# Macaron layer on one core: half-batches instead of batches, quads of heads, fp32 value product in column strips

## Chip, cores, metric

One core of a Trainium2 chip runs the whole program. The metric is device time in microseconds (us), the median of the runs shown.

## What is computed

The input is x with 4 batches of 1024 tokens and 128 features, all in fp32. Three layers follow each other, each on the normalised x:

```python
x = x + 0.5 * ffn(layernorm(x), router_w, router_b, expert_weights)   # first layer, "f = 0"
x = x + attn(layernorm(x), wq, wk_down, wv_down, wk_up, wv_up, wo)    # attention
x = x + 0.5 * ffn(layernorm(x), ...)                                  # last layer, "f = 1"

# ffn: softmax over 8 experts, the best 2, weights normalised; all 8 products x @ E[e] and a gated sum
# attn: 8 query heads of 128, 2 key heads; keys and values are x @ down (32 wide) @ up (32 x 128);
#       causal softmax(q k / sqrt(128)) v, then y @ wo
```

## The kernel before, in words

Keys and values are 32 wide ahead of their up projection, so the kernel folds the up projections into wq and wo. A score then has a contraction of 32, and precision comes from splitting each fp32 factor in a high part (float32r) and a low one: q_stack holds hi, lo, hi of a query head on 96 partitions, k_stack holds hi, hi, lo of a key head. Partitions 96 and 97 of q_stack hold the row maximum (high and low part), those of k_stack hold -1, so that the score matmul subtracts the maximum.

The work of a batch in attention is 96 score blocks: 8 heads, and in each head 12 blocks of 128 keys by up to 512 queries (BLOCKS; 512, 384, 256 or 128 columns, mean 384). For a block there are these steps:

- `maximum` (L1142, and a mask matmul L1145 on the diagonal) makes scores in the other orientation (128 queries by up to 512 keys) in one of 3 banks; the VectorE reduction L935 takes the row maximum into m_part.
- When a head has its 12 maxima, L928 merges them, TensorE transposes them (L1196), ScalarE copies twice (L586), GpSimd takes the low part (L556), and two DMAs put the row into q_stack (L465).
- `scores` (L1157, mask L1160) in one of 2 banks, then ScalarE's exponential L682 into prob (9 buffers of 128 x 512 fp32).
- The low half of prob: prob_lo = prob - upper bf16 half, by GpSimd (L562, three quarters of the blocks) or VectorE (L951).
- `values` (L1180 and L1181): for each 128 queries of the block one matmul with the bf16 upper half of prob as stationary operand and one with the fp16 low half, 97 moving columns each (three bf16 parts of the 32 value columns, and a column of ones that gives the denominator). 36 pieces of 128 queries in a head, so 72 of these matmuls a head and 576 a batch. They accumulate in bank OB; after the last block of 512 queries VectorE makes the reciprocal (L920), the sum of the three parts (L921) and the product (L943, y_lat).

After a batch, `join` transposes y_lat (L1266), ScalarE copies it (yT), and L1277 multiplies with wo; VectorE adds x1_kept (L1009).

The order of the work is written out by hand. Every engine runs the same list of slots, one slot for each of the 96 score blocks (`timeline`, L220 and following), with the offsets of all other steps given in slots: maxima run 20 slots ahead (MAX_LEAD), the row of a head 6 ahead, values 5 to 7 behind. `front(k + 1)` puts the first layer and the projections of the next batch in the slots of batch k, `join` and `back(k - 1)` the output projection and the last layer of the batch before. Batches 1 and 2 are a hardware loop (Fori), batches 0 and 3 are written out; before the first slot comes the whole front of batch 0, and after the last the whole join and back of batch 3.

The first and last layer (ffn) work on tiles of 128 tokens, 8 a batch: statistics (L770, L781), the power and shift by GpSimd (L524, L526), ScalarE's normalisation (L622), transposes (L1079), high and low part, router matmuls (L1101, L1102, 16 and 8 columns), 26 small VectorE instructions for the gates (L820, one set a batch), then two jobs a tile with three float32r matmuls of 512 columns each (L1084 to L1086). ScalarE scales four experts (L661), VectorE adds four (L878), GpSimd joins the sums (L538, L541, L543). The two banks FB serve all of it.

SyncE issues the DMAs that build q_stack and k_stack (L443, L455): 3 a query head and 3 a key head, 30 a batch.

In `prepare_rest` (L1052) stands the only place where matmuls write strips of 32 partitions side by side:

```python
for h in range(NH):
    g, r = divmod(h, NR)
    last = mm(bank[4][r * DL:(r + 1) * DL, g * D:(g + 1) * D], upT[:, DL:2 * DL], wo_sb[:, h, :],
              start=True, stop=True)
```

Of the kernel before, what the change touches and what calls it, by code (L numbers as in the profile page):

```python
# [5 lines left out]
F32 = mybir.dt.float32  # L21
F32R = mybir.dt.float32r
BF16 = mybir.dt.bfloat16
FP16 = mybir.dt.float16
# [5 lines left out]
P = 128  # L30
NT = T // P
CH = 512
NC = T // CH
TC = CH // P
NE = 8
NH, NKV, DL = 8, 2, 32
NR = NH // NKV
NU = NH * NC
# [7 lines left out]
VCOLS = 3 * DL + 1  # L46


BLOCKS = [(c, j) for c in range(NC) for j in range(TC * (c + 1))]

MBLOCKS = [(i, k) for i in range(NT) for k in range(i // TC + 1)]
NBL = len(BLOCKS)
NS = NH * NBL
GS = NS // NKV

MAX_LEAD = 20
ROW_LEAD = 6
PV_LAG = 5
PV_HOLD = 2
NORM_LAG = PV_LAG + 1  # L60
NP = 9

# [4 lines left out]

CUT = 4
JOIN = 7
JOIN_OUT = 11
OUT_STEP = 1
KEEP = 11
STACK_1 = 5
STACK_EVERY = 2
VALUES_1 = 10

BN = [8, 0, 42]  # L80
STATS = [10, 55, 45]
POWER = [12, 55, 47]
XN = [13, 59, 49]
XT = [16, 62, 52]
XHI = [17, 63, 52]
XLO = [17, 64, 53]
XT_STEP = 2

LOGITS = [21, 57]
LOGITS_STEP = [0, 0]  # L90
ROUTE = [22, 59]
ROUTE_SLOTS = [3, 10]
GATE_EXP = [24, 58]
Y = [26, 74]
PACE = [3, 3]
PICK_ACT = 1
PICK_DVE = 1
SPREAD = 0
FINISH = 2
TILE_STATS = 4  # L100

LOAD = 4
PROJ = 68
QUERIES = 69
VALUES = 74
STACK_0 = QUERIES + 3
VALUES_STEP = 0
VALUES_0 = VALUES + 2

HALF = NE // 2  # L110
STAT_SLOTS = 2
# [3 lines left out]
JOBS = 2 * NT  # L115
# [3 lines left out]
def last_block(u):  # L119

    h, c = divmod(u, NC)
    return h * NBL + (TC - 1 if c == 0 else NBL - 1)


UNIT_ENDS = {last_block(u): u for u in range(NU)}


def offset(s):

    c, j = BLOCKS[s % NBL]  # L130
    return max(0, j - TC * c) * P


def diagonal(s):

    c, j = BLOCKS[s % NBL]
    return j >= TC * c


def on_pool(s):  # L140

    return s % NBL not in (0, 3, 6)


def splits(s, pool):

    return sum(on_pool(i) == pool for i in range(s + 1))


def values_slot(s):  # L150

    n = BLOCKS[s % NBL][1]
    return s + max(0, PV_HOLD - n) + PV_LAG


def job_slot(f, j):

    return Y[f] + j // 2 * PACE[f] + j % 2 * (PACE[f] // 2)


def job_at(f, s):

    return next((j for j in range(JOBS) if job_slot(f, j) == s), None)

ENTRIES = []
for _m in range(NS):
    if _m % NBL == MAX_LEAD - NBL - ROW_LEAD:  # L170
        ENTRIES.append(("row", _m // NBL - 1))
    ENTRIES.append(("block", _m))
ENTRY = {e: n for n, e in enumerate(ENTRIES)}


def maxima_bank(entry):

    return MX + ENTRY[entry] % NMX


def entry_before(entry):

    n = ENTRY[entry]
    for back_by in range(1, len(ENTRIES)):
        other = ENTRIES[(n - back_by) % len(ENTRIES)]
        if maxima_bank(other) == maxima_bank(entry):
            return other, back_by > n


def at(k, s):  # L190

    return k + s // NS if s // NS else k, s % NS


def real(b):

    return not isinstance(b, int) or 0 <= b < NB


def is_first(b):  # L200

    return isinstance(b, int) and b == 0


def job_banks(b, f):

    alone = isinstance(b, int) and b == (NB - 1 if f else 0)
    return [FB, FB + 1, MX, MX + 1] if alone else [FB, FB + 1]


def job_bank(b, f, j):
    banks = job_banks(b, f)
    return banks[j % len(banks)]


def need(engine, semaphore, value):

    if not isinstance(value, int) or value > 0:
        engine.wait_ge(semaphore, value)


def timeline(engine, slot, front, join, back):

    for s in range(CUT, CUT + NS):
        front(0, s)

    def run(k, lo, hi):
        for s in range(lo, hi):
            slot(k, s)
            if s >= CUT:  # L230
                if real(k - 1):
                    join(k - 1, s)
                if real(k + 1):
                    front(k + 1, s)
                if real(k - 1):
                    back(k - 1, s)

    run(0, -MAX_LEAD, CUT + NS)
    with engine.Fori(1, NB - 1) as k:
        run(k, CUT, CUT + NS)  # L240
    run(NB - 1, CUT, CUT + NS)
    for s in range(CUT, CUT + NS):
        slot(NB, s)
        join(NB - 1, s)
        back(NB - 1, s)


def macaron(nc, x, wq, wk_down, wv_down, wk_up, wv_up, wo, router_w, router_b, experts, out):
    ctx = ExitStack()
    with ctx:  # L250
# [11 lines left out]

# [3 lines left out]
        mask_kq = sb("mask_kq", [P, P], BF16)  # L266
        rank = sb("rank", [P, NE])
        half_power = sb("half_power", [P, NT])

        wk_up_sb = sb("wk_up_sb", [DL, D])  # L270
        wv_up_sb = sb("wv_up_sb", [DL, D])
        down_sb = sb("down_sb", [P, 2 * NKV * DL])
        rw_sb = sb("rw_sb", [NE, D])
        rb_sb = sb("rb_sb", [P, NE])
        we_sb = sb("we_sb", [P, NE * D])
# [9 lines left out]
        wo_lat = sb("wo_lat", [P, NKV, D])  # L285

        x0 = sb("x0", [P, NT, D])
        x1 = sb("x1", [P, NT, D])
        x1_kept = sb("x1_kept", [P, NT, D])
        x2 = sb("x2", [P, NT, D])  # L290
        x3 = sb("x3", [P, NT, D])
# [109 lines left out]
        def per_expert(ap):  # L401

            return ap.unsqueeze(2).to_broadcast([P, NT, NE])
# [907 lines left out]
```

## Time and profile before

| | us |
|---|---|
| median of 3 runs | 710.64 |
| lowest and highest | 705.13 and 713.25 |
| span of the profiled execution, which is its own time too | 705.1 |
| TensorE / VectorE / GpSimd / ScalarE busy in it | 584.4 / 527.5 / 390.9 / 332.5 |
| mean granted TensorE clock | 0.872 |

The span runs from the first to the last instruction. A TensorE matmul's busy time holds its way through the array too, so the distance between the starts of two matmuls that follow each other says more than a duration. The lines of the page are those of kernel.py.

### The profile page before, as it was taken

The numbers are of one execution on the slowest core, as the hardware profiler recorded it, in microseconds if no ns is written. First come the engines' busy times: TensorE is split into PE (matmuls) and PEld (weight loads), VectorE is DVE, ScalarE is ACT, GpSimd is POOL, SyncE is SP. The second block draws the span as 40 slices with busy tenths as digits, with TensorE's granted clock in tenths as the row PEclk, the third lists the DMA queues.
The fourth block names the chain that finished last, engine by engine and source line by source line (L and its number), as shares of the span: only waits on it lengthen the run. The fifth ranks groups of instructions, "written<-read, shape, count | busy, mean of one in ns | idle before, by whom it ended". The sixth has DMA issues, their size and how long they took to land.

```text
span 705.1 us, 14707 instructions
## 1 busy us (share of the span) xinstructions
PE 584.4 (83%) x4627; PEld 443.5 (63%) x4627; DVE 527.5 (75%) x1454; ACT 332.5 (47%) x885; POOL 390.9 (55%) x549
## 2 busy tenths in 40 slices
PE   3847988989978989888898989888899888898475
PEld 3624666766757856666677756666677667675353
DVE  3553789996788899986796899895787897865243
ACT  4344154655534546553464555554364455355133
POOL 2160164986446549652685559652676575469206
PEclk9986589997989999878898999878699998799857
DMA  4002350000313300004106100003105100000000
GB/s 125 1 1 63 75 148 1 2 2 1 91 24 81 96 2 2 1 2 91 24 3 153 55 1 2 1 2 91 24 3 121 53 2 2 2 2 0 31 0 30
DMA packets 18525, 24.93 MB, mean 35 GB/s; under 512 B 3144, under 2 KB 13968, under 8 KB 18448
## 3 DMA queue, kind: packets, MB, share of 16 engines
q1 hardware_dynamic: 15328, 22.40, 12.9%
q10 hardware_dynamic: 3120, 1.57, 0.8%
q8 instruction: 40, 0.66, 0.4%
q14 instruction: 37, 0.30, 0.1%
HBM read 3.78 MB, written 2.10 MB: 8 GB/s over the span
## 4 chain that ended last, share of the span: by engine, by line
POOL 30%; issue 22%; PE 21%; DVE 19%; ACT 5%; DMA 1%; POOLq 1%; SPq 1%; ACTq 0%; DVEq 0%
POOL prob_lo L562 15%; DVE m_part L935 5%; POOL pair_sum L538 5%; POOL pair_sum L541 4%; PE bank L1142 4%; PE bank L1157 3%; PE bank L1180 3%; PE bank L1181 2%; POOL x L543 2%; POOL rstd L524 2%; DVE prob_lo L951 2%; ACT xn L622 2%; DVE y_lat L943 2%; DVE dve_sum L878 1%; PE bank L1084 1%
## 5 line engine op out<-in xcount | busy, mean ns | idle before, releaser
L562 POOL TENSOR_TENSOR prob_lo<-prob 128x512 f16<-128x512 f32 (+3 forms) x288 | 237.1, 840 | 178.1 <-ACT prob L682 177.5
L682 ACT ACTIVATE prob<-bank 128x512 f32<-128x512 f32 (+3 forms) x384 | 182.8, 487 | 212.0 <-PE bank L1160 191.9
L935 DVE TENSOR_REDUCE m_part<-bank 128x1 f32<-128x512 f32 (+3 forms) x384 | 207.7, 548 | 81.8 <-PE bank L1142 48.2
L1142 PE MATMUL bank<-k_stack,q_stack 96*128 96x512 f32 (+3 forms) x384 | 168.5, 446 | 13.5 <-DVE m_part L935 12.1
L1157 PE MATMUL bank<-q_stack,k_stack 98*128 98x512 f32 (+3 forms) x384 | 166.9, 436 | 8.3 <-ACT prob L682 5.0
L1180 PE MATMUL bank<-v_parts,prob 128*128 128x97 bf16 x1152 | 151.2, 225 | 14.3 <-DVE y_lat L943 13.2
L1181 PE MATMUL bank<-v_parts,prob_lo 128*128 128x97 bf16 x1152 | 149.8, 223 | 0.0
L1180 PEld LDWEIGHTS bank<-v_parts,prob 128*128 128x128 bf16 x1152 | 116.0, 108 | 34.0 <-issue 12.2
L1181 PEld LDWEIGHTS bank<-v_parts,prob_lo 128*128 128x128 f16 x1152 | 117.1, 108 | 0.0
L1142 PEld LDWEIGHTS bank<-k_stack,q_stack 96*128 96x128 f32 x384 | 86.3, 225 | 23.6 <-DVE m_part L935 20.4
L1157 PEld LDWEIGHTS bank<-q_stack,k_stack 98*128 98x128 f32 x384 | 81.5, 212 | 17.5 <-ACT prob L682 6.8
L661 ACT ACTIVATE scaled<-bank,gate 128x128 f32<-128x128 f32 x256 | 72.1, 367 | 28.6 <-POOL x L543 16.5
L1084 PE MATMUL bank<-we_hi,xT_hi 128*128 128x512 f32 x128 | 65.2, 509 | 16.3 <-DVE dve_sum L878 7.7
L538 POOL TENSOR_TENSOR pair_sum<-dve_sum,scaled 128x256 f32<-128x256 f32 x64 | 47.5, 742 | 53.8 <-DVE dve_sum L878 53.8
L951 DVE TENSOR_TENSOR prob_lo<-prob 128x512 f16<-128x512 f32 (+1 forms) x96 | 66.1, 688 | 5.9 <-ACT prob L682 5.8
L1145 PE MATMUL bank<-mask_qk,ident_b 128*128 128x128 bf16 x256 | 64.2, 251 | 0.0
L1160 PE MATMUL bank<-mask_kq,ident_b 128*128 128x128 bf16 x256 | 62.6, 245 | 0.0
L1085 PE MATMUL bank<-we_lo,xT_hi 128*128 128x512 f32 x128 | 54.3, 424 | 0.0
L1086 PE MATMUL bank<-we_hi,xT_lo 128*128 128x512 f32 x128 | 53.9, 421 | 0.0
L622 ACT ACTIVATE xn<-x,shift,rstd 128x128 f32<-128x128 f32 x96 | 40.9, 484 | 25.1 <-POOL shift L526 25.1
L1145 PEld LDWEIGHTS bank<-mask_qk,ident_b 128*128 128x128 bf16 x256 | 27.3, 107 | 35.7 <-issue 26.4
L1160 PEld LDWEIGHTS bank<-mask_kq,ident_b 128*128 128x128 bf16 x256 | 26.6, 104 | 33.9 <-issue 23.4
(132 smaller groups left out, 847.7 us busy)
## 6 DMA issues: line engine op xcount, KB each, us to landing
q_stack<-q_hi SPq DMA_DIRECT2D x64, 128.0 KB, 2.4
q_stack<-q_lo SPq DMA_DIRECT2D x32, 128.0 KB, 2.4
k_stack<-k_hi SPq DMA_DIRECT2D x16, 128.0 KB, 2.5
x_kept<-x SPq DMA_DIRECT2D x4, 512.0 KB, 3.3
out_x<-x SPq DMA_DIRECT2D x4, 512.0 KB, 3.9
x<-in_L_attn_x ACTq DMA_DIRECT2D x3, 512.0 KB, 4.0
k_stack<-k_lo SPq DMA_DIRECT2D x8, 128.0 KB, 2.4
x<-in_L_attn_x SPq DMA_DIRECT2D x1, 512.0 KB, 4.0
```

The source lines that it names most:

```text
L538: nc.gpsimd.tensor_tensor(pair, dve_sum[:, t % 2, 1:3], scaled[:, t % 2, 2:4], ALU.add)\
L562: nc.gpsimd.tensor_tensor(prob_lo[:, ls % NP, 0:w], prob[:, ls % NP, 0:w], upper_half(ls, w), ALU.subtract).then_inc(split_done[True], 1)
L682: nc.scalar.activation(prob[:, ls % NP, 0:w], bank[ST + ls % NST][:, 0:w], ACT.Exp, scale=SCALE).then_inc(p_ready, 1)
L935: V.reduce_max(m_part[:, h, kc, i:i + 1], bank[maxima_bank(("block", ls))][:, 0:w], AX.X)\
L951: V.tensor_tensor(prob_lo[:, ls % NP, 0:w], prob[:, ls % NP, 0:w], upper_half(ls, w), ALU.subtract).then_inc(split_done[False], 1)
L1084: mm(dst, lhs[0], rhs[0], start=True, stop=False)
L1142: last = mm(into[:, 0:w], q_stack[0:MROW, h, i * P:(i + 1) * P], k_stack[0:MROW, h // NR, kc * CH:kc * CH + w], start=True, stop=not diagonal)
L1145: last = mm(into[:, w - P:w], ident_b[:], mask_qk[:], start=False, stop=True)
L1157: last = mm(bank[ST + ls % NST][:, 0:CH - off], k_stack[:, h // NR, j * P:(j + 1) * P], q_stack[:, h, c * CH + off:(c + 1) * CH], start=Tr ...
L1160: last = mm(bank[ST + ls % NST][:, 0:P], ident_b[:], mask_kq[:], start=False, stop=True)
L1180: mm(acc, hi[:, n * P:(n + 1) * P], v, start=first and i == 0, stop=False, skip_group_check=True)
L1181: last = mm(acc, prob_lo[:, ls % NP, n * P:(n + 1) * P], v, start=False, stop=final and i == TC - 1, skip_group_check=True)
```

## The change

The hardware loop goes; all slots are written out, from -70 to 436, with score blocks in slots 0 to 383. The first and last layer and the projections work by half-batches (8 "chunks" n of 512 tokens), each with its own start slot. Attention works by quads, the four heads of one key head for one half of the queries: 4 quads a batch, with 4 or 8 key tiles each, and within a quad key tile by key tile, the four heads one after the other:

```diff
-BLOCKS = [(c, j) for c in range(NC) for j in range(TC * (c + 1))]
+QUADS = [(c, g) for c in range(NC) for g in range(NKV)]
+QTILES = [TC * (c + 1) for c, g in QUADS]
+NPG = 4
+PV_LAG = 3
+ACC_LAG = 2
+DIRECT = 2
...
+def front_start(n):
+    b, c = divmod(n, NC)
+    if b == 0:
+        return (-68, -54)[c]
+    return (b - 1) * NS + (-6, 40)[c]
+
+def back_start(n):
+    b, c = divmod(n, NC)
+    if b == NB - 1:
+        return b * NS + (46, 108)[c]
+    return b * NS + (64, NS + 18)[c]
+
+def join_slot(n):
+    b, c = divmod(n, NC)
+    return b * NS + (40, 104)[c]
```

Relative to its start a chunk has its statistics at +0, the router at +10, the jobs of its four tiles from +15 to +25, and in the front the key projection at +38, the queries at +39 and +40, the values at +41.

The product with the values (TensorE) takes the fp32 probabilities as moving operand and the fp32 values (32 columns) as stationary one; the four heads of a key tile write the four strips of 32 partitions of one bank. prob_lo, v_parts and their instructions are gone:

```diff
-                    mm(acc, hi[:, n * P:(n + 1) * P], v, start=first and i == 0, stop=False, skip_group_check=True)
-                    last = mm(acc, prob_lo[:, ls % NP, n * P:(n + 1) * P], v, start=False,
-                              stop=final and i == TC - 1, skip_group_check=True)
+            def weighted_values(b, q, j):
+                c, g = QUADS[q]
+                off = first_query(q, j)
+                if j == 0:
+                    need(pe, o_copied, b * NQ + q)
+                    pe.wait_ge(v_ready, b * NC + c + 1)
+                pe.wait_ge(p_ready, group_end(b, q, j) + 1)
+                for r in range(NR):
+                    last = mm(bank[OB][r * DL:(r + 1) * DL, off:CH], v_lat[:, b % 2, j, g, :],
+                              probabilities(b, q, j, r), start=j == 0, stop=j == QTILES[q] - 1)
+                last.then_inc(pv_done, 1)
```

The denominators: GpSimd adds the groups of probabilities (key tile 1 up to the third last) into that of key tile 0, two heads in an instruction; TensorE multiplies that sum and the last two groups with a block of ones, in the same four strips, in one of the three banks of the maxima; VectorE transposes 32 x 32 blocks, makes 16 reciprocals a partition and transposes back; ScalarE copies the values' bank, and GpSimd multiplies into yT. With this y_lat and its transposes are gone:

```diff
+            def add_group(b, q, j):
...
+                for half in range(2):
+                    heads = slice(2 * half, 2 * half + 2)
+                    pool.wait_ge(p_ready, group_end(b, q, j) - 1 + 2 * half)
+                    if j > 1:
+                        pool.wait_ge(sum_step, 2 * k - 1 + half)
+                    into = acc[:, (b * NQ + q) % 2, heads, off:CH]
+                    nc.gpsimd.tensor_tensor(into, into, prob[:, home, heads, 0:CH - off], ALU.add)\
+                        .then_inc(sum_step, 1)
...
+            def denominators(Q):
...
+                for j in [0] + list(range(nj - DIRECT, nj)):
+                    for r in range(NR):
+                        last = mm(into[r * DL:(r + 1) * DL, first_query(q, j):CH], ones[:], probabilities(b, q, j, r),
+                                  start=j == 0, stop=j == nj - 1)
...
+                if step == 0:
+                    dve.wait_ge(den_done, Q + 1)
+                    V.transpose(den_t[:], mx_bank(("den", Q))[:]).then_inc(den_step, 1)
```

The maxima of a quad (16 blocks, or 32) have one row step instead of one a head, with one ScalarE copy and the low part by VectorE; they run 38 slots ahead of the batch's first score for three quads, and the fourth quad's in slots 26 to 57. q_stack and k_stack are filled by half-batches, 60 DMAs a batch of half the size each.

## Rows read from the trace of the kernel before

In rows 1 and 10 a line is a stretch: start and end, length, then busy us (and instructions) of TensorE's matmuls, its weight loads, VectorE, ScalarE and GpSimd, then the granted TensorE clock (1 is 2.4 GHz, 0.5 is 1.2 GHz), the DMA share and GB/s. The edges in rows 1 are the starts of the first score matmul of a batch, but for 649 us, which is behind the last.

**Rows 1.** Stretches: prelude, batch 1, batch 3, tail.

```profile
0.00:81.80 81.80, 51.91 (x201) 35.90 (x201) 41.90 (x141) 26.95 (x71) 19.56 (x42) 0.83 0.20 52
...
234.60:392.00 157.40, 138.34 (x1149) 105.87 (x1149) 130.61 (x360) 80.96 (x220) 97.31 (x135) 0.89 0.15 37
...
550.00:649.00 99.00, 87.35 (x788) 66.46 (x788) 76.11 (x199) 49.05 (x129) 63.47 (x83) 0.88 0.03 8
649.00:705.10 56.10, 30.38 (x142) 22.93 (x140) 22.04 (x84) 16.95 (x51) 20.41 (x37) 0.76 0.06 19
```

**Rows 2.** Timeline of TensorE at 301 us: start, duration, line, tile.

```profile
301.63 0.48 PE L1142 MATMUL bank<-k_stack,q_stack 96*128 96x512 f32 x1
301.95 0.22 PE L1157 MATMUL bank<-q_stack,k_stack 98*128 98x128 f32 x1
302.01 0.23 PE L1160 MATMUL bank<-mask_kq,ident_b 128*128 128x128 bf16 x1
...
302.33 0.21 PE L1180 MATMUL bank<-v_parts,prob 128*128 128x97 bf16 x1
302.37 0.21 PE L1181 MATMUL bank<-v_parts,prob_lo 128*128 128x97 bf16 x1
```

**Rows 3.** The same view at 32 us (experts) and 659 us (output projection).

```profile
32.05 0.50 PE L1084 MATMUL bank<-we_hi,xT_hi 128*128 128x512 f32 x1
...
32.86 0.40 PE L1084 MATMUL bank<-we_hi,xT_hi 128*128 128x512 f32 x1
...
659.11 3.84 PE L1277 MATMUL bank<-wo_lat,yT 128*128 128x128 f32 x32 [0.71 <-ACT yT L586]
```

**Rows 4.** Timeline at 24 us: the 16 matmuls of prepare_rest in four strips.

```profile
23.87 0.35 PE L1102 MATMUL bank<-rw_parts,xT_lo 128*128 128x8 f32 x1
...
24.16 1.08 PE L1052 MATMUL bank<-x,upT 128*32 128x128 f32 x16
...
26.19 0.63 PE L1086 MATMUL bank<-we_hi,xT_lo 128*128 128x512 f32 x1
26.61 0.63 PE L1084 MATMUL bank<-we_hi,xT_hi 128*128 128x512 f32 x1
```

**Rows 5.** The same timeline, only those in flight from 24.16 to 24.20 us.

```profile
24.16 0.44 PE L1052 MATMUL bank<-x,upT 128*32 128x128 f32 x4
```

**Rows 6.** Timeline at 318 us: from 128 columns of the array to 64.

```profile
318.02 0.28 PE L1181 MATMUL bank<-v_parts,prob_lo 128*128 128x97 bf16 x1
318.08 0.67 PE L1084 MATMUL bank<-xT_hi,down_hi 128*64 128x512 f32 x1
```

**Rows 7.** Groups by shape on GpSimd and VectorE: count, busy us, mean ns, idle before.

```profile
L562 POOL TENSOR_TENSOR prob_lo<-prob 128x512 f16<-128x512 f32 x128 | 134.0, 1060 | 83.4 <-ACT prob L682 83.3
L562 POOL TENSOR_TENSOR prob_lo<-prob 128x128 f16<-128x128 f32 x32 | 12.8, 400 | 6.2 <-ACT prob L682 5.9
L921 DVE TENSOR_REDUCE o_sum<-bank 128x128 f32<-128x384 f32 x64 | 33.4, 522 | 0.0
L943 DVE TENSOR_TENSOR y_lat<-o_sum,rden 128x128 f32<-128x128 f32 x64 | 33.3, 520 | 1.5 <-PE bank L1266 1.3
```

**Rows 8.** The page's group of VectorE's share of prob_lo.

```profile
L951 DVE TENSOR_TENSOR prob_lo<-prob 128x512 f16<-128x512 f32 (+1 forms) x96 | 66.1, 688 | 5.9 <-ACT prob L682 5.8
```

**Rows 9.** Waits: total us, times, longest.

```profile
PEld bank L1142 <- DVE m_part L935: 20.4, 33, 3.7
PE bank L1180 <- DVE y_lat L943: 13.2, 14, 2.0
PEld bank L1180 <- POOL prob_lo L562: 11.9, 15, 2.1
```

**Rows 10.** Short stretches around the projections, columns as in rows 1.

```profile
324.00:331.00 7.00, 7.00 (x80) 5.74 (x78) 5.37 (x10) 3.21 (x7) 2.41 (x4) 1.00 0.51 116
...
334.60:341.00 6.40, 6.40 (x36) 4.56 (x34) 4.04 (x14) 4.18 (x14) 2.54 (x3) 0.81 0.06 12
```

**Rows 11.** Timeline of SyncE: the issue of one stack DMA.

```profile
327.95 0.59 SPq L443 DMA_DIRECT2D q_stack<-q_hi  x1
```

More of the change, by code:

```diff
@@ L34 @@
 TC = CH // P
+NN = NB * NC
 NE = 8
@@ L114 @@
 N_DMA = 16
-JOBS = 2 * NT
+JOBS = 2 * TC
 CONST_STEPS = 9
[L119 to L153, printed above, removed]
@@ L156, in job_slot @@
[L156 to L187, printed above, removed]
@@ L190, in at @@
[L190 to L213, printed above, removed]
+BN, STATS, POWER, XN, XT, XHI, XLO, LOGITS, ROUTE, GATE_EXP, Y = 0, 1, 3, 5, 7, 8, 9, 10, 11, 12, 15
@@ new lines, in start_of, with chunks_at, quad_of, score @@
+def start_of(f, n):
+    return back_start(n) if f else front_start(n)
+PHASES = sorted(((f, n) for f in range(2) for n in range(NN)), key=lambda p: start_of(*p))
+PHASE = {p: i for i, p in enumerate(PHASES)}
+def chunks_at(f, s, step):
+    return [n for n in range(NN) if start_of(f, n) + step == s]
+def quad_of(ls):
+    return max(q for q in range(NQ) if QSTART[q] <= ls)
+def score(n):
+    b, ls = divmod(n, NS)
+    q = quad_of(ls)
+    j, r = divmod(ls - QSTART[q], NR)
+    return b, q, j, r, max(0, j - TC * QUADS[q][0]) * P
@@ L216, in need @@
+MX_USE = {u: i for i, u in enumerate(MX_USES)}
+FB_USE = {u: i for i, u in enumerate(FB_USES)}
 def need(engine, semaphore, value):
-    if not isinstance(value, int) or value > 0:
+    if value > 0:
         engine.wait_ge(semaphore, value)
[L222 to L245, printed above, removed]
@@ L1012, in back @@
-            def back(b, s):
-                if s == BN[2]:
-                    dve.wait_ge(x2_ready, (b + 1) * NC)
-                norm_piece(b, 2, x2, s)
-                expert_piece(b, 1, s, x2, x3)
-            timeline(dve, slot, front, join, back)
+                        dve.wait_ge(dve_picked, tile * HALF + 1)
+                    V.scalar_tensor_tensor(out=sums[e % 3], in0=fb_bank(("y", f, n, 2 * t + 1))[:, e * D:(e + 1) * D],
+                                           scalar=gate[:, f, n % 2, t, HALF + e:HALF + e + 1], in1=addends[e],
+                                           op0=ALU.mult, op1=ALU.add).then_inc(dve_picked, 1)
@@ L1281, in back, with scores @@
-            def back(b, s):
-                norm_piece(b, 2, s)
-                for c in range(NC):
-                    if s == LOGITS[1] + c * LOGITS_STEP[1]:
-                        router(b, 1, 2, c)
-                if job_at(1, s) is not None:
-                    expert_products(b, 1, job_at(1, s))
-            timeline(pe, slot, front, join, back)
+            def scores(n):
+                b, q, j, r, off = score(n)
+                c, g = QUADS[q]
+                if j == 0 and r == 0:
+                    pe.wait_ge(m_row[q], (b + 1) * 2 * N_DMA)
+                need(pe, p_ready, n - NST + 1)
+                into = bank[ST + n % NST]
+                last = mm(into[:, 0:CH - off], k_stack[:, b % 2, g, j * P:(j + 1) * P],
+                          q_stack[:, c, g * NR + r, off:CH], start=True, stop=not on_diagonal(q, j))
+                if on_diagonal(q, j):
+                    last = mm(into[:, 0:P], ident_b[:], mask_kq[:], start=False, stop=True)
+                last.then_inc(st_done, 1)
```

1349 lines of the change are left out of this document (658 added, 691 removed).

## Prediction

> **What bounds the kernel now.** I read the stretches first, since one mean over the span mixes three regimes [rows 1]: 81.8 us until the first score, three batches of 152.8, 157.4 and 158.0 us (the starts are 81.8, 234.6, 392.0 and 550.0), a last one of 99.0 that has no front to carry, and 56.1 us of tail. In a middle batch TensorE's records cover 138 of 157 us, VectorE's 131, GpSimd's 97, ScalarE's 81. Then the timeline, since a matmul's record is longer than the time in which it blocks the next. At 2.4 GHz starts lie 0.32 us apart behind a score of 512 columns, 0.06 behind one of 128, and 0.04 for the 97 columns of a value matmul, though their records last 0.48, 0.22 and 0.21 [rows 2]. An expert job of three matmuls takes 0.81, a small fp32 matmul 3.84 / 32 = 0.12 [rows 3].
>
> A middle batch by these distances: 576 value matmuls x 0.043 = 24.8 us; 192 scores and maxima, by width 96 x 0.32, 64 x 0.22 (my interpolation for 384 and 256 columns) and 32 x 0.06 = 46.7; 128 masks x 0.045 = 5.8; 32 expert jobs x 0.81 = 25.9; twelve projections of 512 columns x 0.25 and about 128 small matmuls (router, value projection, both kinds of transposes, output) x 0.115 = 17.7. Sum 121 us at full clock. At a granted clock of 0.89 the 157.4 us hold 140 us of full-clock time. So TensorE works 121 of 140, stands 19, and the half clock costs another 17. TensorE bounds the middle; the ends are bound by latency (VectorE 42 and TensorE 52 busy of 81.8, 22 and 30 of 56.1).
>
> The waits that make up the 19 are in part removed by the change [rows 9]: the values wait 13.2 us for y_lat and 11.9 for prob_lo, the maxima 20.4 for VectorE's reductions. Low clock follows stretches of few columns: from 324 to 331 us, at clock 1, the value projection with its 64-column matmuls ends; from 334.6 on it is 0.81 [rows 10].
>
> **The change on TensorE.** It removes 24.8 us of values and 16 transposes of y_lat x 0.115 = 1.8. It adds 96 value matmuls of fp32, in 24 groups of four strips. Do strips run side by side? In prepare_rest four are in flight together, 0.44 us for all four [rows 5], and 16 take 1.08 [rows 4]: (1.08 - 0.44) / 3 = 0.213 us for each round of four. The three-pass neighbours show the low clock there, 0.42 us for 512 columns (26.19 to 26.61) [rows 4], so 128 columns are 0.107 and a round is two cycles a column. A source matmul is two instructions (8 in the source, 16 in the row), so a group of four heads costs four cycles a column: 0.85 us for 512 columns at 2.4 GHz. Columns a batch: quads of 4 key tiles 512 + 384 + 256 + 128 = 1280, of 8 tiles 2048 + 1280 = 3328, together twice each 9216, x 4 / 2.4 = 15.4 us. Denominators: 512 + 256 + 128 = 896 columns a quad, 4 quads, 6.0 us. Bound from the other side: strips in series, four times both.
>
> Entering strips: L1102 starts at 23.87, the strips at 24.16 [rows 4], 0.29 where 0.21 is its own distance at that clock; from full width to 64 columns 318.02 to 318.08 is 0.06 [rows 6], less than the 0.08 of its columns. I take 0.15 us for each of 28 groups (24 and 4), in and out together, 4.2 us; bounds 0 and 0.4 (a record's length beyond its columns, 0.21 - 0.04, twice [rows 2]), so 0 to 11. New load: 121 - 24.8 - 1.8 + 15.4 + 6.0 + 4.2 = 120 us. The value product is no cheaper for the array; the gain must come from waits, clock and ends.
>
> The Trainium skill, TensorEngine Tiling (Array Packing), Key Properties, says that changing the tiling mode drains TensorE. The trace shows 0.08 us and nothing for two such changes [rows 4, 6], so I keep the sum; what the rule would do here at the upper bound's price is rival D.
>
> **The other engines, a middle batch.** VectorE: less 66.1 / 4 = 16.5 for prob_lo [rows 8], 33.4 / 4 + 33.3 / 4 = 16.7 for o_sum and y_lat [rows 7], about 10 for reciprocals, v_parts and m_fin (estimate from their counts, 8 to 64 short ones); plus two transposes of 512 columns a quad at 0.7 (as prob_lo's mean of 0.69 [rows 8]; bounds 0.52, as o_sum, and twice 0.7), 6 us, and the doubled count of small gate and statistic instructions, 73 x 0.2 = 15. 131 - 43 + 22 = 110. GpSimd: an add of two heads has 1024 or 768 elements; 1060 ns for 512 and 400 for 128 give 1.72 ns an element [rows 7], so 1.94 and 1.5 us (bounds: twice 1.06 and twice that again, if fp32 output or VectorE's port slows it). A batch has 16 long and 8 short ones, 43 us. Removed are 72 splits of 384 columns in the mean, 0.40 + 256 x 0.00172 = 0.84 each, 60 us, and eight low parts of a row at about 0.5. With normalise (four of 512 elements, 4.2) and more power steps (3, estimate) it ends near 97 - 64 + 50 = 83. ScalarE keeps its exponentials, near 80. None of the three passes TensorE. SyncE goes from 30 to 60 stack DMAs a batch at 0.59 [rows 11], 36 us of issue, beside everything. Behind a chunk's 30 DMAs (18 us, some 13 slots) waits the row of the next quad; rows are asked for 5 to 21 slots ahead of their scores, so I count 0, and 5 us a batch if the queue is late.
>
> Added waits: values wait for a whole group of exponentials, 3 slots behind the last, behind them on TensorE the next scores; 3 slots are 4 us against 0.6 for an exponential, hidden. The exponential of a group waits for GpSimd's add of the group 4 back, 12 slots later. Where tiles finish (three GpSimd instructions of 256, 128 and 128 elements, by the same line 0.6 + 0.4 + 0.4 = 1.4 us every 3 slots) and 8-tile quads are summed (3.9 every 4 slots), GpSimd needs 5.8 us in 4 slots of 1.5, about all of them, but only for 12 slots at a time, and the four buffers hold that.
>
> **The period.** Full-clock idle 19: less (13.2 + 11.9) / 4 = 6.3 for the removed waits, less half of 20.4 / 4 as VectorE falls from 0.83 of the period to 0.76, plus 2 for the denominators' and quads' hand-overs: 12. Router and value projection come in halves, with scores between, so stretches of few columns are shorter; I put the clock at 0.91 (bounds 0.75 and 0.97). (120 + 12) / 0.91 = 145 us against 152.8 to 158.0.
>
> **The ends.** Prelude: routing and experts of chunk 1 stand ahead of chunk 0's projections in the order, and the first quad needs 18 DMAs (11 us) and 16 maxima where a head needed 6 and 12. Half the first layer saved, about as much put back: 78 (bounds 70 to 88) for 81.8. Last batch: less than 99.0, since more maxima lie ahead, though chunk 6's last layer is now in it: 96. Tail: 56.1 falls to four tiles: statistics, eight transposes less, four experts less (about 2 us a tile, estimate from two jobs of 0.81 [rows 3] and their hand-over) but the whole gate chain; 39 (34 to 46).
>
> Sum 78 + 3 x 145 + 96 + 39 = 648 for the profiled execution. It has 705.1 where the median is 710.64, 5.5 more; forecast 654.
>
> **Rivals.**
> A, the forecast, 0.43: 625 to 682.
> B, 0.20: the waits only change their names and the clock stays; (120 + 19) / 0.89 = 156 a batch, 78 + 468 + 100 + 39 = 685, 690 with the offset. For it: PE's expert banks and the order of the slots stay, and VectorE stays at 0.7 to 0.8.
> C, 0.13: 6 idle at 0.97 is 130; 78 + 390 + 86 + 38 = 592, 597. For it: no wait in the middle is needed by the loads; against: 0.89 in every batch.
> D, 0.08: each change of width drains the array, at the 0.17 us that a record runs beyond its columns [rows 2]: 11 us with the rounding up a batch in place of 4.2: (127 + 14) / 0.91 = 155; 692 at the end.
> E, slower, 0.12: TensorE falls to the low clock while it runs strips and small groups between short waits. At 0.75 a batch takes (120 + 12) / 0.75 = 176: 78 + 528 + 116 + 40 = 762, 767. It turns the sign from a mean clock of about 0.82 down, where 132 / 0.82 = 161 eats what the ends give. For it: the clock drops behind few-column stretches [rows 10]; against: rounds of strips move as many columns a cycle as full-width ones.
> F, slower, 0.04: the strips run in series because 512 columns of fp32 from four buffers differ from 128 of one; 64 us more a batch, over 900. Against: rows 5.
>
> **Chances.** Faster by over 1%: A, C, nearly all of B and D, 0.79; within 1% 0.06 (the upper edge of B and D; about what a measurement can tell); slower 0.15. Range 594 to 718: below lies 0.05 of C, above E and F. A's own is 625 to 682.
>
> **What would show it.** In the profile after: value groups 0.85 us apart for 512 columns at clock 1, eight instructions each (else F); no gap over 0.15 at their edges (else D); mean clock in the middle 0.9 (else E); GpSimd's 1024-element add near 1.94 us; VectorE 110 a batch; batch starts 145 apart; first score at 78, 39 from last score to end. If periods of 156 appear with the loads as worked out, the idle term was wrong.

## The result and the profile after

The changed kernel takes 798.68 us (median of 4, 792.26 to 802.26) where the kernel before, run beside it, takes 707.88 (median of 4, 699.29 to 713.25): a ratio of 1.130, 95% interval 1.124 to 1.136. The forecast was 654 with a range up to 718. The sign was wrong and the range did not hold the time. All times below leave out the executions of a second, slower state (a lower granted clock and a longer time, whatever the kernel), so that den_pe stands at 746.4 us and tiny_rows at 708.0 where the expectations name the medians of all their executions, 752.95 and 708.87.

The stretches of the profiled execution of the changed kernel (span 800.4 us), cut at the first score of each batch and at the last score; columns as in [rows 1]:

```profile
0.00:100.00 100.00, 54.19 (x216) 37.82 (x216) 50.03 (x189) 28.36 (x74) 22.29 (x47) 0.78 0.26 67
100.20:266.80 166.60, 138.24 (x779) 82.45 (x779) 122.43 (x317) 72.84 (x186) 80.73 (x72) 0.84 0.10 23
266.80:454.60 187.80, 156.43 (x840) 95.03 (x839) 130.18 (x362) 79.97 (x211) 89.84 (x89) 0.78 0.11 28
454.60:637.50 182.90, 155.36 (x841) 94.69 (x840) 125.16 (x351) 79.97 (x210) 85.69 (x85) 0.78 0.11 26
637.50:753.00 115.50, 102.03 (x642) 57.80 (x641) 67.52 (x185) 59.54 (x146) 68.84 (x58) 0.88 0.06 15
753.00:800.00 47.00, 20.56 (x90) 13.22 (x86) 14.05 (x58) 7.96 (x24) 15.60 (x19) 0.68 0.02 6
```

For a comparison the kernel before has to be divided in the same way. The edges 234.6, 392.0 and 550.0 of [rows 1] are not first scores: the trace has 384 score matmuls, and those that open batches 1, 2 and 3 start at 215.8, 367.8 and 527.1 us, the last at 645.0. Divided there, its batches take 134.0, 152.0, 159.3 and 117.9 us, not 152.8, 157.4, 158.0 and 99.0, and its tail 60.1, not 56.1. The two in the middle:

```profile
215.80:367.80 152.00, 135.46 (x1146) 103.84 (x1145) 129.16 (x355) 79.54 (x215) 93.20 (x127) 0.90 0.14 35
367.80:527.10 159.30, 141.22 (x1148) 108.70 (x1146) 130.01 (x360) 80.96 (x219) 97.38 (x135) 0.87 0.15 37
```

So the prelude grew by 18 us and the first three batches by 33, 36 and 24; the last shrank by 2 and the tail by 13. In the middle batch, against 234.6 to 392.0 of [rows 1] (also 96 score blocks), TensorE's busy time rose from 138 to 156 us, but at a clock of 0.78 in place of 0.89: 156 x 0.78 = 122 against 138 x 0.89 = 123. By this rough measure the array has the same work as before. What rose is waiting and time at the low clock. On GpSimd the additions stand where the splits stood [rows 7]:

```profile
L509 POOL TENSOR_TENSOR acc<-acc,prob 128x1024 f32<-128x1024 f32 x64 | 149.6, 2365 | 17.9 <-ACT prob L639 16.6 <-PE bank L1095 1.4
L509 POOL TENSOR_TENSOR acc<-acc,prob 128x768 f32<-128x768 f32 x32 | 57.4, 1814 | 32.8 <-PE bank L1095 32.0 <-ACT prob L639 0.8
```

TensorE's own rows in the view of waits (who waited for whom) sum to 166 us (111 before). The longest groups, where [rows 9] had the values' waits for y_lat and prob_lo, which are gone:

```profile
PE bank L1004 <- ACT xn L573: 32.4, 16, 6.2
PE bank L1062 <- DVE m_part L833: 21.5, 12, 6.3
PE bank L990 <- DVE g_r L759: 16.8, 5, 7.5
PE bank L990 <- ACT scaled L598: 12.4, 8, 3.6
PE bank L990 <- DVE dve_sum L806: 11.5, 10, 1.6
PE bank L1062 <- DVE mT_lo L698: 10.2, 5, 4.1
PE bank L1075 <- DMA q_stack<-mT_lo: 10.0, 1, 10.0
PE bank L1062 <- DMA q_stack<-q_hi: 8.9, 1, 8.9
```

The columns are total us, times, longest. The third is put down to the gate's g_r, though its longest waits are those of a key projection (7.5 and 4.2 us), which asks for xT_lo: this stands on VectorE behind the gate chain. The timeline shows why that chain is late. First GpSimd, then VectorE, then TensorE, the changed kernel at 358 to 373 us:

```profile
358.32 15.73 POOL L509 TENSOR_TENSOR acc<-acc,prob 128x1024 f32<-128x1024 f32 x7
```

```profile
364.30 1.11 DVE L759 TENSOR_TENSOR g_s<-g_l,g_r 128x32 f32<-128x32 f32 x1
365.44 2.29 DVE L759 SCALAR_TENSOR_TENSOR g_k<-g_s,rank 128x32 f32<-128x32 f32 x1
367.76 0.19 DVE L759 TENSOR_REDUCE g_r<-g_k 128x4 f32<-128x32 f32 x1
367.99 2.04 DVE L759 TENSOR_TENSOR g<-g_k,g_r 128x32 f32<-128x32 f32 x1
370.06 2.26 DVE L759 SCALAR_TENSOR_TENSOR g<-g,g_s 128x32 f32<-128x32 f32 x1
372.25 0.68 DVE L833 TENSOR_REDUCE m_part<-bank 128x1 f32<-128x512 f32 x1
```

```profile
372.98 0.80 PE L1062 MATMUL bank<-k_stack,q_stack 96*128 96x512 f32 x1 [6.30 <-DVE m_part L833]
```

Operations over 32 columns that take 0.19 us alone take up to 2.29 us here, the length of an addition, while additions run (one took 5.58 us at 179 us); the reductions, with one input, keep their 0.19 and 0.68. Behind them the reduction of a maxima block is late, and TensorE stands for 6.30 us. Its clock falls towards the end of this wait:

```profile
360.00:366.00 6.00, 6.00 (x42) 3.06 (x41) 4.67 (x10) 2.91 (x8) 6.00 (x4) 1.00 0.05 14
366.00:373.00 7.00, 0.69 (x7) 0.31 (x3) 6.90 (x7) 0.92 (x3) 7.00 (x4) 0.80 0.00 0
373.00:383.90 10.90, 9.33 (x31) 5.53 (x32) 9.29 (x29) 2.08 (x7) 4.02 (x4) 0.50 0.00 0
```

After the wait the array works for 10.9 us at 1.2 GHz (0.50 of 2.4). The excess, summed over the gate's and the statistics' small operations of VectorE, as the time beyond the least that each kind takes, is 78.3 us in 584 instructions, 22.7 in 292 before.

### The profile page after: what moved, and what is told of

The parts are those of the page before. It is cut to its first block and busy times, and to the rows that moved or that the text cites. A ratio compares the mean times of both kernels' runs of the same rounds, so it can differ in the third digit from the quotient of the medians.

```text
span 800.4 us, 10467 instructions
## 1 busy us (share of the span) xinstructions
PE 626.9 (78%) x3395; PEld 381.0 (48%) x3395; DVE 509.4 (64%) x1462; ACT 328.6 (41%) x849; POOL 363.0 (45%) x365
## 5 line engine op out<-in xcount | busy, mean ns | idle before, releaser
L639 ACT ACTIVATE prob<-bank 128x512 f32<-128x512 f32 (+3 forms) x320 | 145.5, 472 | 237.1 <-PE bank L1078 175.0
L509 POOL TENSOR_TENSOR acc<-acc,prob 128x1024 f32<-128x1024 f32 (+1 forms) x96 | 206.8, 2181 | 50.7 <-PE bank L1095 33.4
L833 DVE TENSOR_REDUCE m_part<-bank 128x1 f32<-128x512 f32 (+3 forms) x256 | 144.4, 583 | 65.9 <-PE bank L1062 37.6
L833 DVE TENSOR_REDUCE m_fin<-bank 128x1 f32<-128x128 f32 (+3 forms) x128 | 60.6, 484 | 80.1 <-PE bank L1065 79.7
L1095 PE MATMUL bank<-prob,v_lat 128*32 128x512 f32 (+3 forms) x640 | 78.4, 568 | 0.4 <-ACT prob L639 0.4
L518 POOL TENSOR_TENSOR yT<-o_sb,r_t 128x512 f32<-128x512 f32 x16 | 20.4, 1278 | 112.8 <-DVE dve_sum L806 57.4
L639 ACT ACTIVATE acc<-bank 128x512 f32<-128x512 f32 x64 | 38.3, 599 | 70.5 <-PE bank L1078 38.3
L473 POOL TENSOR_TENSOR rstd<-var_eps,half_power 128x4 f32<-128x4 f32 x24 | 24.3, 1014 | 71.4 <-DVE neg_mean L727 71.4
L990 PEld LDWEIGHTS bank<-we_hi,xT_hi 128*128 128x128 f32 x128 | 29.5, 231 | 52.5 <-issue 19.8
L1004 PE MATMUL bank<-ident,xn 128*128 128x128 f32 x96 | 20.9, 359 | 32.8 <-ACT xn L573 32.4
```

The source lines that it names most:

```text
L509: nc.gpsimd.tensor_tensor(into, into, prob[:, home, heads, 0:CH - off], ALU.add)\
L639: nc.scalar.activation(into, bank[ST + n % NST][:, 0:w], ACT.Exp, scale=SCALE).then_inc(p_ready, 1)
L833: V.reduce_max(into, mx_bank(("block", m))[:, 0:w], AX.X).then_inc(mx_red, 1)
L990: mm(dst, lhs[0], rhs[0], start=True, stop=False)
L1095: last = mm(bank[OB][r * DL:(r + 1) * DL, off:CH], v_lat[:, b % 2, j, g, :], probabilities(b, q, j, r), start=j == 0, stop=j == QTILES[q] - 1)
```

## The experiments

Theories: P, the additions keep VectorE's two-input operations waiting; Q, the row of maxima is late on SyncE's queue; S, the order by half-batches itself costs the time. Each kernel starts from the changed one. The times are medians; "waits" (the sum of TensorE's rows in the view of waits), the mean granted clock and "clocked" (span times clock) are those of the one profiled execution. The ratio is to the kernel before, run beside it, with its 95% interval.

| kernel | us | ratio | waits | clock | clocked |
|---|---|---|---|---|---|
| before | 707.88 | 1 | 111 | 0.872 | 615 |
| after | 798.68 | 1.130 (1.124-1.136) | 166 | 0.802 | 642 |
| tiny_adds | 718.82 | 1.015 (1.010-1.020) | 120 | 0.862 | 616 |
| rows_act | 789.38 | 1.113 (1.106-1.120) | 163 | 0.809 | 636 |
| tiny_rows | 708.0 | 0.998 (0.993-1.003) | 111 | 0.852 | 607 |
| den_pe | 746.4 | 1.050 (1.040-1.060) | | | |
| busy_pool | 716.30 | 1.013 (1.005-1.022) | 123 | 0.864 | 618 |
| busy_long | 742.8 | 1.046 (1.032-1.059) | 132 | 0.829 | 616 |
| half_adds | 742.17 | 1.047 (1.035-1.059) | 127 | 0.827 | 617 |
| chopped_adds | 808.51 | 1.139 (1.130-1.148) | 173 | 0.791 | 638 |
| paced_adds | 805.6 | 1.146 (1.138-1.154) | 173 | 0.808 | 646 |
| paced_rows | 795.35 | 1.127 (1.120-1.134) | 166 | 0.821 | 650 |
| dve_rows | 785.34 | 1.111 (1.105-1.116) | 142 | 0.799 | 630 |
| den_pe_rows | 743.99 | 1.053 (1.044-1.061) | 113 | 0.888 | 656 |
| pairs | 796.03 | 1.125 (1.116-1.134) | 129 | 0.825 | 655 |
| warm | 799.35 | 1.123 (1.116-1.131) | 150 | 0.844 | 674 |
| den_warm | 764.1 | 1.069 (1.060-1.079) | 100 | 0.898 | 685 |

**tiny_adds, rows_act, tiny_rows.**

```
-  into = acc[:, (b * NQ + q) % 2, heads, off:CH]               # tiny_adds
-  nc.gpsimd.tensor_tensor(into, into, prob[:, home, heads, 0:CH - off], ALU.add)
+  into = acc[:, (b * NQ + q) % 2, heads, off:off + 2]
+  nc.gpsimd.tensor_tensor(into, into, prob[:, home, heads, 0:2], ALU.add)

-  if s in ROW_AT: stack_maxima(ROW_AT[s])       # SyncE          rows_act
+  if s - 1 in ROW_AT: stack_maxima(ROW_AT[s - 1])   # ScalarE
```

> Leaves out nearly all of the sums of the probabilities: each of GpSimd's additions of a group runs over 2 columns per head instead of up to 512, so the denominators cover only two columns of every later group; all waits, their order and the rest stay. Theory P (the additions hold up VectorE's operations with two inputs in SBUF): the additions' 206.8 us go, the gate chain's products, up to 2.07 us beside an addition, are all near their least of 0.19 us, the 78 us of excess of those operations falls below the 23 us of the kernel before, the waits on pair_sum and yT for VectorE shrink, and the time falls by 50 to 110 us, to 690-750. Theory Q (SyncE's queue: the row of maxima lies behind 30 transfers of a half-batch): the prelude stays at 100 us and the time falls by under 20, to 780-800. Theory S (the order by half-batches itself makes the engines wait for each other): under 10 us, 790-800.

> The two transfers of each quad's row of maxima are issued by ScalarE one slot later, instead of by SyncE; nothing is left out. Theory Q: the row no longer lies behind SyncE's 30 stacking transfers; the first score block starts some 8 to 10 us earlier (100.2 to about 91 us), the batches gain 5 us each, and the time falls by 15 to 30 us, to 770-785. Theory P: the prelude gains, the batches stay at 167 to 188 us: 785-800. Theory S: within 5 us of 798, since ScalarE pays for the issue of 8 transfers a batch what SyncE saved.

> Both edits together: additions over 2 columns per head (the sums of the probabilities left out as in tiny_adds) and the rows of maxima on ScalarE's queue. Theory P with Q: the gains add, 50 to 110 us of the one and 10 to 30 of the other: 670-735. Theory P alone: the same as tiny_adds within 10 us. Theory S: 780-800.

Theory P came out as put: 798.7 - 718.8 = 79.9 us go with the additions, and the excess on VectorE falls to 12.7. Q is right in the prelude only: the first score starts at 92.1 instead of 100.2 us, and the gain is 9.3 us (about 11 on top of tiny_adds), not 15 to 30. In the changed kernel the first row stands behind the last of SyncE's stacking transfers and lands 10.0 us after TensorE asked for it:

```profile
96.37 0.59 SPq L419 DMA_DIRECT2D q_stack<-q_lo  x1
97.01 0.58 SPq L419 DMA_DIRECT2D q_stack<-q_hi  x1
97.63 0.59 SPq L426 DMA_DIRECT2D q_stack<-mT_hi  x1
98.26 0.59 SPq L426 DMA_DIRECT2D q_stack<-mT_lo  x1
```

Both together are within 1% of the kernel before. So even with the sums free nothing is won by the rest of the change. It is not idle, though: by the same stretches tiny_rows (profiled span 713.0) loses 10 us in the prelude and 16, 10 and 1 in the first three batches, and wins 9 in the last batch and 20 in the tail.

**busy_pool and busy_long: is it what an addition reads, or how long it is?**

```
   # tiny_adds, and ahead of each addition:
+  for _ in range(4 if off == 0 else 3):        # busy_long: 6 and 4
+      need(pool, busy_step, busy_count[0])
+      nc.gpsimd.memset(busy[:], 0.0).then_inc(busy_step, 1)
+      busy_count[0] += 1
```

> As tiny_adds (each addition runs over 2 columns per head, so the sums of the probabilities are left out), but ahead of each one GpSimd clears 128x256 elements of a tile that nobody reads, four times (three times ahead of the shorter additions), each waiting for the one before: some 2.0 to 2.4 us, about the length of the addition that it stands for, in which GpSimd reads nothing from SBUF. Theory P1 (an addition harms by what it reads: VectorE's operations with two inputs in SBUF wait while it runs): the gate chain stays near 0.19 us an operation and the time stays near that of tiny_adds, 718.8: 710-735. Theory P2 (an addition harms by its length: GpSimd comes late to its other work): the time returns to that of the changed kernel, 780-800. If clearing also holds VectorE up, the gate chain's excess returns too, and with it the time.

> As busy_pool, with 6 clearings (4 ahead of the shorter additions) instead of 4 and 3: in busy_pool the stand-in for an addition took only 1.6 us (four clearings in 1.42 us and 0.20), where the addition takes 2.37. Now it takes 2.3 (1.6), the addition's own length, still without reading SBUF, and the sums are left out as before. Theory P1 (an addition harms by what it reads): 712-728, as busy_pool's 716.3. Theory P2 with a threshold (GpSimd's queue comes late once its additions are full length): 770-800.

busy_pool's 716.3 speaks for P1, but its stand-in was too short: 1.6 us for 2.37, not the 2.0 to 2.4 that I had put. In busy_long it has the addition's length:

```profile
344.72 2.16 POOL L513 MEMSET busy<- 128x256 f32 x6
346.84 0.23 POOL L515 TENSOR_TENSOR acc<-acc,prob 128x4 f32<-128x4 f32 x1
```

It took 742.8, between the two theories: 742.8 - 718.8 = 24 us of the 80 come back by GpSimd's length alone, with VectorE's excess at 12.5. Against tiny_adds TensorE's waits rise by 11 us, about half of them waits for xn, which needs GpSimd's rstd and shift (34.5 in tiny_adds, 40.1 here). The other 798.7 - 742.8 = 56 come only with additions that read SBUF; with intervals of over 1% on each time the parts are known to some 10 us. Clearing does not hold VectorE up.

**half_adds.** The additions of heads 2 and 3 run over 2 columns.

> The additions of heads 0 and 1 of each group of four are whole, those of heads 2 and 3 run over 2 columns (their sums are left out): half of the additions' time. Between tiny_adds (718.8) and the changed kernel (798.7). If every addition costs alike, half the loss: 755-765. If what harms is several additions in a row, through which VectorE waits (up to 5.58 us in the changed kernel), well under half: 722-745. If a few us of lateness at one place decide, most of it remains: 775-795.

742.2: the first half of the additions costs 23 us, the second 57. That is in the range of "several in a row" (722 to 745), near its upper edge. The longest of the gate's operations on VectorE is 2.37 us instead of 5.58, and the excess 33 us. The cost grows faster than the time of the additions.

**chopped_adds, paced_adds, paced_rows.**

```
   # in short; chopped_adds has the same pieces without need(), and one then_inc behind the last
-  nc.gpsimd.tensor_tensor(into, into, prob[...], ALU.add).then_inc(sum_step, 1)
+  for i in range(2):
+      for n, lo in enumerate((0, 256)):
+          hi = min(lo + 256, CH - off)
+          need(pool, sum_step, 8 * k + 4 * half + 2 * i + n)
+          part = into[:, i, lo:hi]
+          nc.gpsimd.tensor_tensor(part, part, prob[:, home, 2 * half + i, lo:hi], ALU.add).then_inc(sum_step, 1)
```

> Nothing is left out: each addition of two heads is issued in pieces of 256 or 128 columns of one head (four pieces of 0.73 us each by the row of pair_sum, 2.9 us, where one instruction took 2.37). Theory P1 with waits for the instruction in progress: an operation of VectorE waits at most one piece, so its longest falls from 2.07 to about 0.8 us, the excess of the gate and statistics operations from 78 to about 30 us, and the time to 740-775. Theory P2: GpSimd is busy 50 us longer in all and everything is later: 800-815. If a held-up operation waits until GpSimd pauses, and not for one instruction, the longest waits stay over 2 us: 795-815.

> Nothing is left out: the additions in the pieces of chopped_adds (808.51 us), but each piece waits for the end of the one before by a semaphore, so that GpSimd pauses between them. Theory P3 (GpSimd keeps VectorE out from one instruction to the next as long as they follow without a pause; in chopped_adds one operation of 128x32 took 10.35 us, to the end of a chain of 18 pieces): the longest waits fall to one piece, under 1.7 us, although GpSimd's busy time is the same, and the time falls to 750-785. Theory P4 (what counts is the total time of the additions, however they are spaced): longest waits over 3 us again and 795-815.

> paced_adds and the rows of maxima on ScalarE's queue: another 9 to 10 us off paced_adds, all ahead of the first score block, if the two causes are independent: 740-776; not below 709, the time without the sums (tiny_rows 708.87).

Chopping took 808.5, which both the third alternative and P2 allow; the longest waits decide for the third. GpSimd's chain and one operation of VectorE in chopped_adds:

```profile
353.93 12.34 POOL L513 TENSOR_TENSOR acc<-acc,prob 128x256 f32<-128x256 f32 x18
```

```profile
355.96 10.35 DVE L764 TENSOR_TENSOR g_s<-g_l,g_r 128x32 f32<-128x32 f32 x1
```

The chain ends at 366.27, the operation at 366.31: it waited through some fifteen instructions, not one. The Trainium skill (SBUF — State Buffer, SBUF: two separate sides) says that a VectorE operation with two SBUF inputs and a GpSimd operation that reads SBUF exclude each other for the whole instruction. The trace agrees on who is held up; here it lasted through a chain of instructions, beyond what the page says.

With pauses between the pieces the longest of the gate's operations took 0.77 us, one piece, so P3's mechanism is shown. Yet the time stayed at 805.6, and P3's number is a miss. Two things stand in the trace. The excess on VectorE is still 50 us (78.3 in the changed kernel, 12.7 in tiny_adds): the waits are short now, but there are many. And GpSimd is busy 419 us in place of 363, and TensorE waits for it through xn:

```profile
PE bank L1007 <- ACT xn L576: 48.7, 16, 6.6
```

In part one wait was traded for the other (32.4 us of these in the changed kernel); how the time divides between the two was not separated. paced_rows is 10 us faster than paced_adds; its 795 also missed the 740 to 776.

**dve_rows.** The function of the additions is moved as it is from GpSimd's program to VectorE's, on top of rows_act.

> Nothing is left out: the additions, whole, are moved from GpSimd to VectorE (before its reductions in the same slot), rows of maxima on ScalarE's queue. An estimate from VectorE's 341 ns for 128x128 and 681 ns for a reduction of 128x512: 1.1 us for 1024 elements, 24 additions a batch, 24 us more of VectorE (109 to 133 us of a batch of 160), and no additions of GpSimd for it to wait for. Theory P: 709 of tiny_rows plus what VectorE's load costs in waits, 715-745. If VectorE's queue becomes what TensorE waits for: 750-780.

785.3, above both. The additions took 1283 and 996 ns there, no operation waits for GpSimd any more (excess 12.9), but VectorE is busy for 135 us of a 183 us batch where tiny_rows has 109 of 162. The sums cannot ride on either engine.

**den_pe, den_pe_rows, pairs.**

```
   # den_pe: weighted_values, ahead of the strips of the values; no additions
+  if j == 0: need(pe, den_step, 3 * (b * NQ + q) - 2)
+  for r in range(NR):
+      mm(bank[DB][r * DL:(r + 1) * DL, off:CH], ones[:],
+         probabilities(b, q, j, r), start=j == 0, stop=j == QTILES[q] - 1)
   # pairs: den_pe_rows, and both groups of a pair in the second one's slot
-  PV_AT[group_end(*_g) + PV_LAG] = _g
+  PV_AT.setdefault(group_end(_b, _q, _j | 1) + PV_LAG, []).append(_g)
```

> Nothing is left out: the denominators of every group come from TensorE again, four strips with the ones as weights just before the group's value matmuls, into a bank of their own (the maxima keep two banks instead of three); GpSimd adds nothing. It also makes mT_lo ahead of the reductions in VectorE's slot. Array work a batch rises by 5632 columns of four strips, in rounds of 0.427 us for 512 columns: 5632/512 x 4 x 0.213 = 9.4 us at the full clock, 40 us in all with the clock of this kernel, less what the separate denominators took. Theory P: VectorE is free of the additions, which gives 50 to 110 us, less up to 35: 710-780. Theory Q or S: nothing is won and the array work is added: 810-840.

> Both remedies that leave nothing out: the denominators of every group on TensorE (den_pe, 752.95 us) and the maxima's rows on ScalarE's queue (rows_act, -9.3 us; of tiny_rows against tiny_adds -9.9). Theory Q (the row waits for SyncE in the prelude alone): 740-748, all of the gain ahead of the first score block, which starts at 92 us where den_pe's started at 101.8. If the denominators' four strips are the bound of the batches now, the same. It does not beat the kernel before in either.

> den_pe_rows, and the strips of two key blocks (j and j+1) are issued back to back, in one stretch, instead of four score slots apart: half as many entries from full-array work into strips, as many loads of weights for strips. Theory M (the 0.2 to 0.3 us ahead of a group of four strips is the change between full-array work and strips): 24 entries a batch fewer at 0.25 us, 6 us a batch, 20-25 us in all: 718-728. Theory W (it is the loading of the four strips' weights, which nothing hides; in den_pe a group of values straight behind its denominators still started about 0.3 us late): within 5 us of den_pe_rows. If the values come too late for the normalisation at a quad's end, slower by up to 10.

den_pe gives 52 us, den_pe_rows 55, both in the ranges of P and Q. With two executions behind den_pe (741.6 and 751.1) the 2 us between them say nothing about the rows. den_pe_rows is the fastest version here that leaves nothing out, and it still loses to the kernel before by 5.3%. Its array works more (4 x 9.4 us at full clock), and its waits are as low as before's.

In pairs theory M is right that the edges cost and the weights do not, and no theory is right about the time. Entries into strips and out of them, in the changed kernel, and strips behind strips in pairs:

```profile
305.69 0.47 PE L1062 MATMUL bank<-k_stack,q_stack 96*128 96x512 f32 x1
306.10 1.06 PE L1095 MATMUL bank<-acc,v_lat 128*32 128x512 f32 x8
307.09 0.44 PE L1075 MATMUL bank<-q_stack,k_stack 98*128 98x384 f32 x1
```

```profile
345.54 1.04 PE L1094 MATMUL bank<-acc,v_lat 128*32 128x512 f32 x8
346.39 1.04 PE L1091 MATMUL bank<-prob,ones 128*32 128x512 f32 x8
347.25 1.04 PE L1094 MATMUL bank<-prob,v_lat 128*32 128x512 f32 x8
```

Strips behind strips with other weights start 0.85 us apart, the bare columns, so the weights cost nothing. From full width the group here starts 0.41 us behind a maximum of 512 columns. Full-width neighbours of such a maximum start 0.23 to 0.24 us behind it (20 of 95 at full clock) or 0.31 to 0.34 (72), strips 0.32 to 0.33 (9 of 21) or 0.40 to 0.43 (12): 0.09 us for like with like, 0.17 at the most. On the way out it is 0.99 for 0.85, so 0.14. But pairs took 52 us more than den_pe_rows. The middle batches, den_pe_rows first:

```profile
250.90:415.70 164.80, 143.55 (x937) 83.40 (x935) 109.13 (x362) 79.55 (x210) 38.52 (x64) 0.93 0.13 32
```

```profile
263.30:447.50 184.20, 157.91 (x936) 94.04 (x936) 108.61 (x363) 79.53 (x211) 38.46 (x65) 0.82 0.12 28
```

164.8 x 0.93 = 153 and 184.2 x 0.82 = 151: the full-clock time hardly changed, and the batch took 19 us more beside a lower clock. TensorE's waits rose by 16 us in the whole kernel. Why the clock fell so far was not found.

**warm and den_warm: is the clock itself the loss?**

```
   # transposes(2, n), ahead of its wait: 10 times; key_projection(n), n > 0: 12 times
+  mm(into, we_hi[:, 0:P], we_hi[:, 0:CH], start=True, stop=True)
```

> The changed kernel (798.68 us) with nothing moved or left out, and matmuls that nobody reads added at two points of TensorE's program where it stands waiting: 10 of 512 columns ahead of the wait for xn in the transposes of the second router's chunks, and 12 ahead of the wait for xT_lo in each key projection, written into the bank that is overwritten next; 44 x 0.213 us = 9.4 us of array work more in a batch. In the middle batch of the changed kernel TensorE waits 3.22, 1.62 and 4.24 us there, and the clock's low stretches at 312-329, 401-411 and 414-435 us start at or within 1 us after three of these waits. Theory K (two thirds of the loss is the clock: a wait of some us is followed by a stretch at 1.2 GHz): the waits are filled, some 40 of the 82 us at the low clock go, 20 us a batch less 2 to 4 of uncovered filling: 730-770. Theory L (the lateness itself is the loss, and the clock follows from something else, the strips or the load): 800-835, by up to 9.4 us a batch.

> den_pe_rows (743.99 us) with the same filling. Its middle batch has 21 us at the low clock in six short stretches, and waits of 1.60 and 1.66 us at the filled points: theory K gives at most 5 us a batch and takes back 6 of uncovered filling: 738-760. Theory L: 755-775.

The clock rose to 0.844, and the low clock's part of the middle batch fell from 82 to 52 us, but the time did not move. The 35 us of filling (164 matmuls of 0.213) appear as 32 more clocked us. Other waits stayed, among them 6.8 us for a probability at 372 us, which nothing filled. So raising the clock with extra work is no remedy, and theory K's 730 to 770 is refuted for this filling. den_warm lost 20 us, in L's range; warm's 799.35 is just under L's 800. What a higher clock would bring without added work was not tried.

## Why the prediction was wrong, step by step

**The array's load** was right within the edges of strips: 121 us became 120 in the sum, 123 became 122 by busy time and clock. Groups of four strips run 0.85 us apart; rival F is refuted.

**The edges of strips** were taken at 0.15 us a group with bounds 0 and 0.4: they measure 0.23 to 0.31, so 28 groups make 6.4 to 8.7 us instead of 4.2. I had set aside the Trainium skill's rule (TensorEngine Tiling (Array Packing), Key Properties: changing the mode drains) for two rows of narrow tiles. The trace agrees with it in so far as both edges cost time; that the time is a drain no run shows. Rival D was nearer in this, but it is 2 to 4.5 us a batch of full-clock time and not the sign.

**GpSimd's addition** was put at 1.94 and 1.5 us: 2.37 and 1.81, so 90 us a batch rather than 83.

**VectorE** was put at 110 us a batch. Without the additions it is 109.0 (tiny_rows), with them 130. Here is the step that failed: "None of the three passes TensorE". I had named the port and asked only what it does to the length of GpSimd's own addition. I did not ask what an addition of 2.4 us, seven or eight in a row, does to VectorE's operations beside it, nor who stands behind these on VectorE's queue: the reductions and xT_lo that TensorE waits for. That is some 56 of the 80 us. The other 24 come with GpSimd's own length, in part as its lateness for rstd and shift; "four buffers hold that" looked at the probabilities alone.

**SyncE**, "I count 0": the middle was nearly right, but the first quad's row has no lead. TensorE waits 10.0 us for it once, and 8 of them come back ahead of the first score when ScalarE issues it.

**The idle term and the clock** were the second failure. For tiny_rows, with the sums free, I would have forecast 654 as well, and it takes 708. Its span of 713 against my 648 is: prelude 92 for 78, middle batches 149.7, 162.2 and 159.8 for 145 each (37 us in all), last batch 109 for 96, tail 39.8 for 39. TensorE waits 19.6 us in its middle batch, 18.9 before: the removed waits for y_lat and prob_lo came back under other names, as rival B had it, and the clock stayed at 0.87 instead of rising to 0.91. I had subtracted waits without asking what was late next. Theory S holds that much: the rest of the change is worth nothing, within 1%. The last batch is also a misreading: its 96 was set against 99.0, and from first score to last the kernel before has 117.9. For the three batches ahead of it the forecast of 3 x 145 = 435 stood against 445 and not 468, so 10 us were to be gained there, where tiny_rows loses 26. Which part of the change gives the loss in the prelude and in the first two batches was not separated.

**Rival E** had the sign, the break-even clock of 0.82 (measured 0.78), and came nearest in time (767 for 799). Its mechanism was not the one: den_pe_rows has more strips and a clock of 0.93 in its middle batch. Over these kernels the low clock goes with TensorE's waits (111 us at 0.872, 166 at 0.802) rather than with its strips; pairs, with 129 us at 0.825 and 52 us more than den_pe_rows, shows that the waits' sum alone does not give it. By clocked time of the profiled executions, 95 us more span are 27 us of it, 31 us at 0.872; the other 64 stand beside the lower clock. In the same way busy_long and half_adds take 24 and 23 us more than tiny_adds, and in clocked time, by the medians over their executions, 12 and 6 (627 and 621 against 615). That is an accounting; warm shows that it cannot simply be bought back.

**Sums.** Two do not come out. D's terms (78 + 3 x 155 + 96 + 39, and 5.5) make 684, not 692, and E and F together have 0.16, not 0.15. Neither bears on the forecast.

## What to carry to other kernels

Work moved to GpSimd that reads SBUF is not free because GpSimd has room: count VectorE's two-input operations beside it, however small, and follow who waits behind them on VectorE's queue. Half of the additions cost 23 of the 80 us and the second half 57; shorter pieces without pauses did not help; pauses cut the longest wait but left most of their sum, and made GpSimd itself later. If a wait is removed from a queue that runs in order, look for what becomes late next before it is subtracted, and price a new wait of several us on TensorE at more than its length: here the wait of 6.3 us was followed by 10.9 us at 1.2 GHz, and 55 us more of waits stood beside 95 us more of time. To check a reading of stretches, count the instructions: the edges here were off by 14 blocks.

## What the runs showed of the hardware

- One VectorE operation of 128x32 with two inputs in SBUF took 10.35 us, to the end of GpSimd's unbroken chain of additions (chopped_adds). Reductions and operations with an input in PSUM did not change beside additions (0.19 and 0.34 us, changed kernel). GpSimd's clearing of SBUF held up nothing (excess 12.5 us in busy_long, 12.7 in tiny_adds).
- fp32 matmuls of 512 columns run four at a time in four column strips at the full rate of each (0.85 us for the four, at 2.4 GHz), and new weights for the strips cost nothing between groups (pairs). Going in costs 0.09 to 0.17 us and coming out 0.14 (changed kernel).
- An addition of two SBUF inputs of 1024 elements takes 2.37 us on GpSimd (changed kernel) and 1.28 on VectorE (dve_rows).
- Matmuls placed to fill TensorE's waits (warm) raised the mean granted clock from 0.802 to 0.844, and the time stayed the same.
